# Routed rows scattered one at a time, and the first image's outputs weighed and turned by 128 tokens per expert tile

## The reference, cut to what matters

```
x = x + conv_block(norm(x))            # 4 dilations, softmax filters, projection, group norm, relu
t = tokens(x);  z = layer_norm(t)
logits = z @ router.T;  p = softmax(logits)
(p1, e1), (p2, e2) = top_2(p);  g = p / (p1 + p2)
y_e = gelu(z @ w1[e] + b1[e]) @ w2[e] + b2[e]
out = t + z + g1 * y_e1 + g2 * y_e2    # back to channels x pixels
```

## Time and profile before

| | |
|---|---|
| time, median of 3 runs | 2258.05 us (2256.24 to 2268.76) |
| span of the profiled execution | 2561.4 us; no time beside the span is given for it |
| PE, DVE, ACT, POOL busy | 79%, 61%, 52%, 43% of the span |
| mean granted clock of TensorE | 0.863 |
| DMA | 459.86 MB, mean 180 GB/s |

### The profile page before, as it was taken

One profiled execution on the slowest core, in us unless ns is written; L12 is line 12 of the kernel. 1 busy time (PEld: TensorE's weight loads), 2 busy tenths in 40 slices (PEclk: granted clock), 3 DMA queues, 4 the chain that ended last, 5 costly groups with the idle time before them and its releaser, 6 DMA issues.

```text
span 2561.4 us, 56574 instructions
## 1 busy us (share of the span) xinstructions
PE 2032.5 (79%) x20204; PEld 1920.6 (75%) x20204; DVE 1571.4 (61%) x4176; ACT 1336.8 (52%) x2869; POOL 1102.4 (43%) x1466
## 2 busy tenths in 40 slices
PE   5798899999699798878777776766676758988853
PEld 5788899999699787777777766666675657888842
DVE  5667665666577566546555554665665646766765
ACT  4576443333477545444444426665564637777732
POOL 4567122322276513433444442455655554444420
PEclk9899899999899888888787887887876869999975
DMA  5642455676443265556566567554554436777879
GB/s 172 220 127 76 140 157 144 166 174 172 119 142 111 81 192 176 161 163 170 183 181 182 157 213 237 164 171 154 174 174 152 152 121 228 252 257 255 276 267 369
DMA packets 340865, 459.86 MB, mean 180 GB/s; under 512 B 82749, under 2 KB 261437, under 8 KB 338237
## 3 DMA queue, kind: packets, MB, share of 16 engines
q1 hardware_dynamic: 229696, 245.14, 33.8%
q10 hardware_dynamic: 68433, 109.55, 12.8%
q0 software_dynamic: 42464, 101.56, 11.6%
HBM read 291.86 MB, written 174.69 MB: 182 GB/s over the span
## 4 chain that ended last, share of the span: by engine, by line
PE 47%; ACT 16%; another core or an unknown queue 9%; issue 8%; DVE 7%; DMA 6%; POOL 3%; ACTq 3%; SPq 1%; POOLq 1%; DVEq 0%
PE ps_y L426 15%; PE ps L426 7%; PE ps_a L426 6%; PE ps_o L1064 6%; PE ps_b L1001 4%; ACT e_act L1468 3%; ACT w_now L1479 3%; DMA o_acc<-res_scratch 2%; POOL taps L2147 2%; ACT h_hi L1471 1%; PE ps_tok L895 1%; PE ps_o L1051 1%; PE ps_k L846 1%; PE ps_a L939 1%
## 5 line engine op out<-in xcount | busy, mean ns | idle before, releaser
L426 PE MATMUL ps_y<-cat_hi,wp 128*128 128x288 f32 x2048 | 504.4, 322 | 10.9 <-issue 9.0
L2205 POOL DMA_INDIRECT expert_out<-e_out,e_dest x320 | 327.7, 1024 | 414.0 <-DVE e_out L2027 350.2
L2183 POOL DMA_DIRECT2D patches<-rows_scratch x348 | 194.7, 603 | 609.9 <-PE ps_o L1051 405.8
L426 PEld LDWEIGHTS ps_y<-cat_hi,wp 128*128 128x128 f32 x2048 | 370.6, 203 | 17.9 <-issue 15.9
L2127 POOL DMA_INDIRECT expert_in<-r_ln,r_pos x288 | 286.1, 993 | 114.0 <-issue 86.2
L2147 POOL TENSOR_TENSOR taps<-taps,g_rows 96x108 f32<-96x108 f32 (+3 forms) x440 | 259.9, 617 | 166.5 <-ACT g_rows L1303 162.6
L426 PE MATMUL ps<-w,h_hi 128*128 x1280 | 271.5, 309 | 75.7 <-DVE h_lo L2016 47.4
L1941 DVE SCALAR_TENSOR_TENSOR cat_lo<-ps_o,cat_hi 128x288 fp32r<-128x288 f32 (+1 forms) x576 | 228.0, 419 | 161.0 <-ACT cat_hi L1423 131.2
L426 PE MATMUL ps_y<-cat_lo,wp 128*128 128x288 f32 x1024 | 317.3, 310 | 6.3 <-issue 6.2
L1417 ACT ACTIVATE bands<-ps_b 112x288 f16<-112x288 f32 (+4 forms) x256 | 105.1, 411 | 406.3 <-PE ps_b L1001 325.9
L426 PE MATMUL ps<-e_hi,w_now 128*128 128x256 f32 x1280 | 283.9, 303 | 26.2 <-issue 21.3
(11 more groups left out here) (202 smaller groups left out, 4656.6 us busy)
## 6 DMA issues: line engine op xcount, KB each, us to landing
e_x<-expert_in SPq DMA_DIRECT2D x160, 260.0 KB
patches<-rows_scratch SPq DMA_DIRECT2D x160, 192.0 KB
patches<-rows_scratch SPq DMA_DIRECT2D x256, 108.0 KB
patches<-rows_scratch SPq DMA_DIRECT2D x192, 112.0 KB
x_in<-in_x SPq DMA_DIRECT2D x48, 384.0 KB, 3.6
rows_scratch<-rows_st SPq DMA_DIRECT2D x48, 384.0 KB, 4.3
r_x<-in_x ACTq DMA_DIRECT2D x72, 256.0 KB
r_y<-y_scratch ACTq DMA_DIRECT2D x72, 256.0 KB
```

Of the source, the lines that this page charges most:

```text
L426: mm = eng.matmul(out, lhs[p], rhs[q], start=start and n == 0, stop=stop and n == 2)
L2183: pool.dma_start(patch_target(s, n), patch_source(m, s, n)).then_inc(patch_pooled[s % RING], 16)
L2205: pool.indirect_dma_start(out=ys_dram, out_offset=bass.IndirectOffsetOnAxis(ap=e_dest[:, i, j:j + 1], axis=0), in_=e_out[:, u, j], in_offs ...
```

## The change

Four things are changed.

1. In the convolution stage of image 1, the twelve scatters of a pair are begun one at a time: scatter k of pair p waits until PE has done unit `placed(p) + 1 + 3k//2`. Before the patch loads of a step POOL sends those scatters whose unit is less than the unit that the loads wait for.
2. Between the expert tiles of image 0, the row scatters go singly behind each of the two sends of a tile: scatter k of pair p behind half-tile `2 * (placed(p)//4 - 1) + 4k//5`. The last one goes with tile 73.
3. The outputs of image 0 are weighed and turned by 128 tokens per tile: part k of group g is weighed first at tile 87 + 3g + k, second one tile later, turned three later, and the group is written at tile 92 + 3g; its loads begin at tile 81 + 3g. `o_summed` now counts parts. The turning of the last two parts and the write of the last group come behind the last product.
4. In the tail the same single parts are used: the weighing order is unchanged, and PE turns each part once it is summed.

```diff
-        def out_group_at(n):
-            g = (n - OUT_FIRST) // 3
-            return g if n >= OUT_FIRST and (n - OUT_FIRST) % 3 == 0 and g < GROUPS_OUT else None
+        def out_part_at(n):
+            g, k = divmod(n - OUT_FIRST, TT)
+            return (g, k) if 0 <= g < GROUPS_OUT else None
...
-            def turn_out(g):
+            def turn_out(g, k):
                 u = 0 if g < GROUPS_OUT else g % 2
-                pe.wait_ge(o_summed, g + 1)
-                after(pe, o_copied, g if g <= GROUPS_OUT else g - 1)
-                for k in range(TT):
-                    for c in range(CC):
-                        mm = pe.transpose(...)
-                mm.then_inc(o_turned, 1)
+                pe.wait_ge(o_summed, g * TT + k + 1)
+                if k == 0:
+                    after(pe, o_copied, g if g <= GROUPS_OUT else g - 1)
+                for c in range(CC):
+                    mm = pe.transpose(...)
+                if k == TT - 1:
+                    mm.then_inc(o_turned, 1)
...
             second_product(STREAM - 1)
+            for n in range(STREAM, STREAM + 3):
+                part = out_part_at(n - 3)
+                if part is not None:
+                    turn_out(*part)
...
-                if n >= OUT_FIRST - 3 and sent < GROUPS_OUT and sent <= (n - OUT_FIRST + 3) // 3 + OB - 2:
+                if n >= OUT_FIRST - 3 and sent < GROUPS_OUT and sent <= (n - OUT_FIRST + 3) // 3 + OB - 3:
                     load_outputs(sent)
...
-            def scatter_rows(p, q):
-                if q == 0:
-                    pool.wait_ge(r_placed, p + 1)
-                    pool.wait_ge(r_lnd, TP * (p + 1))
-                for k in range(4 * q, 4 * q + 4):
-                    t, z = divmod(k, TOP)
-                    pool.indirect_dma_start(...)
+            def scatter_row(p, k):
+                t, z = divmod(k, TOP)
+                if k == 0:
+                    pool.wait_ge(r_placed, p + 1)
+                if z == 0:
+                    pool.wait_ge(r_lnd, TP * p + t + 1)
+                pool.indirect_dma_start(...)
...
+                def scatter_unit(i):
+                    p, k = divmod(i, ROWS_OUT)
+                    return plans[0].placed(p) + 1 + 3 * k // 2
+                def paced_scatters(sent, before_unit):
+                    while sent < CPAIRS * ROWS_OUT and scatter_unit(sent) < before_unit:
+                        pool.wait_ge(out_ready, m * UNITS + min(scatter_unit(sent), UNITS))
+                        scatter_row(*divmod(sent, ROWS_OUT))
+                        sent += 1
+                    return sent
...
                 for s in range(1, STEPS):
                     shared = [n for n in range(loads(s)) if second_queue(s, n)]
+                    free_at = unit(s - RING + 1) if s >= RING else 0
+                    if m:
+                        sent = paced_scatters(sent, free_at)
                     if shared and s >= RING:
-                        pool.wait_ge(out_ready, m * UNITS + unit(s - RING + 1))
+                        pool.wait_ge(out_ready, m * UNITS + free_at)
                     for n in shared:
                         pool.dma_start(...)
-                    while m and thirds < 3 * CPAIRS and scatter_step(thirds // 3, thirds % 3) <= s:
-                        scatter_rows(thirds // 3, thirds % 3)
-                        thirds += 1
...
+            def scatter_half(i):
+                p, k = divmod(i, ROWS_OUT)
+                return 2 * (plans[1].placed(p) // 4 - 1) + 4 * k // 5
+            sent = 0
             for n in range(STREAM):
-                send(n)
-                while thirds < 3 * CPAIRS and scatter_after(thirds // 3, thirds % 3) <= n:
-                    scatter_rows(CPAIRS + thirds // 3, thirds % 3)
-                    thirds += 1
+                for j in range(S // 128):
+                    send(n, j)
+                    while sent < CPAIRS * ROWS_OUT and scatter_half(sent) <= 2 * n + j:
+                        p, k = divmod(sent, ROWS_OUT)
+                        scatter_row(CPAIRS + p, k)
+                        sent += 1
```

More of the change, by code:

```diff
@@ L68 @@
 XROWS = IMAGES * XBLOCK
+ROWS_OUT = TP * TOP
 EARLY = 5
@@ L1169, in _ @@
             second_product(STREAM - 1)
+            for n in range(STREAM, STREAM + 3):
+                part = out_part_at(n - 3)
+                if part is not None:
+                    turn_out(*part)
             for g in range(GROUPS_OUT, 2 * GROUPS_OUT):
-                turn_out(g)
+                for k in range(TT):
+                    turn_out(g, k)
         @block.scalar
@@ L1554, in _ @@
                     gate_exponents(r)
-                g = out_group_at(n - 3)
-                if g is not None:
-                    write_out(g)
-                if n >= OUT_FIRST - 3 and sent < GROUPS_OUT and sent <= (n - OUT_FIRST + 3) // 3 + OB - 2:
+                part = out_part_at(n - 3)
+                if part is not None and part[1] == TT - 1:
+                    write_out(part[0])
+                    written += 1
+                if n >= OUT_FIRST - 3 and sent < GROUPS_OUT and sent <= (n - OUT_FIRST + 3) // 3 + OB - 3:
                     load_outputs(sent)
                     sent += 1
-            for g in range(GROUPS_OUT, 2 * GROUPS_OUT):
+            for g in range(written, 2 * GROUPS_OUT):
                 write_out(g)
@@ L2050, in gates @@
                 dve.tensor_tensor(gate[:, 1, here], soft1[:, 5], soft1[:, 2], ALU.mult).then_inc(gate_done, 1)
[L2052 to L2059, removed]
-                for k in range(TT):
-                    t = g * TT + k
-                    rest = res_early[:, g - GROUPS_OUT, k] if early(g) else o_acc[:, n, k]
-                    dve.scalar_tensor_tensor(out=o_acc[:, n, k], in0=o_y[:, n, k, 0], scalar=gate[:, 0, t:t + 1],
-                                             in1=rest, op0=ALU.mult, op1=ALU.add).then_inc(o_first, 1)
@@ L2077, in _, with weigh_second @@
+            def weigh_second(g, k):
+                n, t = g % OB, g * TT + k
+                if k == 0:
+                    after(dve, o_turned, g - 1)
+                dve.wait_ge(o_first, t + 1)
+                dve.scalar_tensor_tensor(out=o_sum[:, g % 2, k], in0=o_y[:, n, k, 1], scalar=gate[:, 1, t:t + 1],
+                                         in1=o_acc[:, n, k], op0=ALU.mult, op1=ALU.add).then_inc(o_summed, 1)
             input_lo(0)
@@ L2098, in _ @@
                     gates(n // ETILES)
-                g = out_group_at(n)
-                if g is not None:
-                    weigh_first(g)
-                g = out_group_at(n - 1)
-                if g is not None:
-                    weigh_second(g)
+                part = out_part_at(n)
+                if part is not None:
+                    weigh_first(*part)
+                part = out_part_at(n - 1)
+                if part is not None:
+                    weigh_second(*part)
             output(STREAM - 1)
             for g in range(GROUPS_OUT, 2 * GROUPS_OUT):
-                weigh_first(g)
-                weigh_second(g)
+                for k in range(TT):
+                    weigh_first(g, k)
+                for k in range(TT):
+                    weigh_second(g, k)
         @block.gpsimd
```

62 lines of the change are left out of this document (28 added, 34 removed).

## The result

| | before | after |
|---|---|---|
| time, median (runs) | 2258.24 us (4) | 2300.84 us (4; 2294.3 to 2302.5) |
| ratio, 95% interval | | 1.0173, 1.0146 to 1.0200 |
| span of the profiled execution | 2561.4 us, and 2254.9 us in a second one | 2298.5 us |

The prediction was 2253 us with a range up to 2272: wrong, and on the other side. The span fell by 263 us, the median rose by 42. The profiled execution of after took 2300.32 us, 1.8 us over its span: this profile is one of the timed kind. All comparisons from here on go by this second profile; the first is returned to at the end.

The account below looks back on a forecast made before the run. It took POOL's scatters to pace image 0's expert tiles and most late signals to come from recording. Terms 0 - 4 + 0 + 0.5 - 1.0 = -4.5 us took the 2258 us median to 2253 us, range 2212 to 2272.

Parts of the forecast that it names:

- The weight of the late signals: Whole profile: 367 us of late signals, mostly from recording; at most 64 us of their kind in timed runs.
- The sum by it, 1891 us: Whole kernel: by the skill's 6.2 us rule all 367 us could be won, time down to 1891 us; not used.
- Part two: Row scatters between image 0's expert tiles: POOL sets the pace, spreading helps only at the queue's end, -4 us.
- the rival of the row buffers: Image 0's expert tiles: ACT's copy waits for the later last row, about 3 us for 9 pairs, 2285 us; chance 0.15.
- Both signs that I had named: Profile after: ACT waiting before its row-buffer copy on a scatter; POOL idle before scatters between tiles 20 and 70.
- The room that I weighed this against, 11.2 us: Row buffers: 11.2 us, less the landing, from a pair's last row issue to the copy that takes its buffer again.
- Part one: Single scatters in the second convolution stage: 0 in the timed run, at most 21 us loss or a share of 64 gain.
- Part three: Outputs of image 0 between image 1's expert tiles: same work, ACT's 11.13 us per three tiles not lessened, 0 us.
- ACT's 1.6 us wait: Second expert stage, per three tiles: a late signal of the 303 us; whole wait, 38 us, bounds the gain.
- Part four: The end: later store of the last group +0.5 us, last turning partly under the sums -1.0 us.
- Slower: Whole kernel: chance of a loss, 0.15 for row buffers and 0.02 for patch loads that come late.

Follow-up runs that it names:

- e8: Kernel before plus 60 pairs of small POOL memsets at tiles 11 to 70, on a chip where before takes 2554.07 us: 2553.65 us, ratio 1.0000.
- e13: Kernel before plus two small POOL memsets (120 in all) behind the second send of each of tiles 11 to 70: 2272.82 us, ratio 1.0055.
- e4: Kernel before with only the paced single scatters of the convolution stage: 2259.72 us, ratio 0.9995.
- e15: Kernel after with the last pair's rows begun closer together, its last row with tile 70 instead of 73: 2298.17 us, ratio 1.0170.
- e6: Kernel after with single rows between expert tiles wider apart, row k behind half-tile k instead of 4k//5: 2331.17 us, ratio 1.0311.
- e3: Kernel before with only the changes to image 0's outputs and the tail: 2263.51 us, ratio 1.0015.
- e5: Kernel after with single rows closer, row k behind half-tile k//2, so a pair's last row keeps its place of before: 2261.98 us, ratio 1.0018.
- e7: Kernel after with two signals for each row buffer, one for its first three tiles and one for the others: 2268.91 us, ratio 1.0036.
- e16: Kernel after with two signals for each row buffer and the last pair's last row with tile 70 instead of 73: 2261.08 us, ratio 1.0002.
- e9: Kernel after plus 60 pairs of small POOL memsets, on the chip where before takes 2554.07 us: 2413.58 us, ratio 0.9438 to before.

## Why the prediction was wrong, step by step

**The weight of the late signals: wrong, and it fed the rest.** I had read the 303 us between span and median as the recording's doing. A second recording of the same kernel has a span 2.0 us under its own time and no wait put down to "remote", and on another chip the runs that nobody recorded take 2554 us against 2258, with a profile (e8) that is full of such waits. So the late signals go with the chip, or with its condition in that job, and not with the recording. That the first profile was taken on such a chip is the likely reading of its 2561 us; no run shows which chip it was. The Trainium skill (Runtime: NRT & Kernel Launch, The ~15µs preamble/postamble breakdown) has a profile's total stand about 6.2 us over the reported time whatever the kernel. Here neither the size nor the side agrees: the spans of all the other profiles stand 1.8 to 2.2 us under the times of their own executions. But a small gap that is the same for every kernel is what this case has too, and 303 us are nothing like it. Taken seriously, that would have said that this profile and these times were not of one condition. The sum by it, 1891 us, would have been wrong all the same.

**Part two is the step that failed**: "Spreading cannot help a queue that is never empty", minus 4 us, and against the rival of the row buffers, "with POOL always busy this wait takes the place of another one". It measured +42 us. That POOL bound this stage was right in the main (85% of the chain, and 29.7 / 5.25 = 5.7 us a tile where I had 5.6; e13 has POOL as more than half of the bound). But a queue is only never empty as long as those who fill it are not held by it. The row buffers close a ring: row scatter, landing, ACT's copy, gelu, result, POOL. The last row stands in the program's order behind the sends of later tiles, and those wait for the results that ACT can't make. Both signs that I had named for this came: ACT's waits with a row scatter as releaser, and idle time of POOL in this stage. The room that I weighed this against, 11.2 us, came from a profile whose signals were late; in the second profile it is the landing and 0.9 us more. The rival had the mechanism and the sign. Its price, 3 us a pair, measured 3.9 (33.5 in after, 29.6 in e4), 35 us in nine pairs; 2 to 5 more are the last row's hold on image 1's first load (e15), which I hadn't seen. The rest, up to 5 us, no run tells from the scatter. An estimate after the fact: a ring that spans three pairs hands on a third of a delay to each. After delays the last row by 1.5 tiles (I had written two) of 33.5 / 5.25 = 6.4 us, a third of which is 3.2 us a pair; e6 by 3 tiles of 6.9 us, thus 6.9 us. Measured 3.9 and 6.7.

**Part one: right in size, by the timed runs** (e4: 0.9995). POOL's row scatters of that stage now stand between waits for PE, as I had said:

```profile
1092.88 0.97 POOL L2134 DMA_INDIRECT expert_in<-r_ln,r_pos  x1 [0.30 <-issue]
1095.77 0.97 POOL L2134 DMA_INDIRECT expert_in<-r_ln,r_pos  x1 [1.92 <-PE ps_o L1052]
1098.33 0.97 POOL L2134 DMA_INDIRECT expert_in<-r_ln,r_pos  x1 [1.59 <-PE ps_o L1052]
```

**Part three: 0 was right** (e3: 1.0015), and ACT's 1.6 us wait was no part of the timed runs, as I had said. In before's second profile ACT begins the activation 0.05 us after it has issued the last load; the 1.63 us of idle time are its own three issues:

```profile
1906.17 0.80 ACT L1494 ACTIVATE o_out<-ps_t 128x768 f32<-128x768 f32 x1
...
1907.93 0.62 ACTq L1513 DMA_DIRECT2D o_acc<-res_scratch  x1
1908.60 0.84 ACT L1468 ACTIVATE e_act<-ps,b_of 128x256 f32<-128x256 f32 x2 [1.63 <-issue]
```

That profile has 20 such lumps of issues, 1.8 us each, in image 1's tiles (first rows); after, which splits them over two tiles, has mostly waits on PE in their place (second rows):

```profile
ACT e_act L1468 <- issue: 36.4, 20, 2.0
ACT e_act L1468 <- PE ps L426: 13.8, 16, 3.2
```

```profile
ACT e_act L1475 <- PE ps L427: 34.3, 56, 1.7
ACT e_act L1475 <- ACT o_out L1501: 10.2, 22, 0.5
```

The stage stays at 299 us with PE busy 283 of them in both kernels. I read it so that the smoothing took the lump away and PE was the floor under it; no run shortened PE's work to show that.

**Part four: the piece as expected, the time unchanged.** I had the last turning run under the sums, -1.0. It does. The first of the last three sums ends at 2293.20 (the row below is all three), PE begins 0.05 us later and is through 0.8 us after the last of them; in before's second profile, as in the earlier trace rows, it begins behind the last sum and is through 1.6 us after it:

```profile
2292.72 1.27 DVE L2079 SCALAR_TENSOR_TENSOR o_sum<-o_y,gate,o_acc 128x256 f32<-128x256 f32 x3
```

```profile
2293.25 1.54 PE L1143 MATMUL ps_t<-ident,o_sum 128*128 128x128 f32 x6 [2.30 <-DVE o_sum L2079]
```

But the tail is 103.6 us in both kernels, so neither these 0.8 us nor the 0.5 us that I gave the later store show in the time.

**The chances.** Slower had 0.17, and the range stopped at 2272 although the rival's own sum was 2285. I had bounded the wait by the room in one profile, and hadn't asked what the room would be without the late signals, the profile's largest entry.

## What to carry to other kernels

In this kernel a full queue went empty because those who feed it waited for one of its own late entries. So before spreading transfers, list what each landing releases, and keep the last one of each group where it was (e5), or give the buffer finer signals (e7, e16). Spreading then cost next to nothing here (2 us in e5, none that shows in e16), but where the timed runs take 2258 us it also gave nothing. And where a profile's span is 13% over the timed runs, record again before reading waits from it: rooms and shares from such a profile don't hold for the runs that are timed.

## What the runs showed of the hardware

- The same kernel took 2258 to 2261 us (medians) on the other chips and 2554 us, timed, on the chip of e8 and e9. By e8's stages most of the difference lies where POOL scatters: the second convolution stage and image 0's tiles, with signals between engines arriving late, as in the first profile of before (13.6 us in the earlier trace rows). TensorE's granted clock there was 0.84 and 0.80, against 0.97 and 0.91.
- On that chip the changed kernel with memsets has a span 140 us shorter than before with memsets (2400.0 against 2540.2); by stage lengths as in the table 114 of it are in the second convolution stage (507.2 against 621.6), 14 in image 0's tiles (545.1 against 559.2) and 9 in image 1's (304.9 against 313.5). The first is where scatters were spread out singly with pauses. That the pauses are the cause is argued only: no run on that chip had part one alone.
- An indirect scatter of 128 rows of 1040 bytes took 5.9 us from issue to landing (1651.10) with other scatters begun 1.3 to 1.8 us apart around it. It is not a constant: the last rows of after's nine pairs have 3.7 to 6.0 us to the copy that waits for them, those of e6 have 2.5 to 3.1 us.
- Issuing one cost POOL 1.0 us and a gap of 0.3 us, with its rows singly or four in a row (1037 ns in after, 1015 in e4).
